# An attention layer with a mixture of experts on one core: new orders at four places, and a front with the keys' bias as a column of the weights' product, the high parts of u first, the output bias added by VectorE, and statistics moved

## The chip, the core and the metric

The kernel runs on one core of a Trainium2 chip. Five engines work from queues of their own and meet at semaphores: TensorE (PE, matmuls and transposes into PSUM), VectorE (DVE), ScalarE (ACT, activations and scaled copies), GpSimd (POOL), and SyncE (SP, which here only issues transfers). The metric is the device time of one execution in microseconds (us), lower is better. A median over several executions is given beside one profiled execution.

## What is computed

```python
x = L0_attn_x                                   # (4, 1024, 256), float32
xn = _layernorm(x, axis=-1)
q, k, v = xn @ Wq.T + bq, xn @ Wk.T + bk, xn @ Wv.T + bv
qk = q @ k.T                                    # no scaling
theta = 0.5 + 0.2 * sigmoid(qk) + 0.15 * tanh(qk) + 0.1 * relu(qk)
s = softmax(theta) @ v @ Wo.T + bo
expert = argmax(xn @ Wr + br)                   # one of 8 per token
y = gelu(xn @ W1[expert] + b1[expert]) @ W2[expert] + b2[expert]   # hidden width 1024
out = x + s * silu(y)
```

## The kernel before

**Arithmetic.** Every large product is made from two-part numbers: a high part in TensorE's reduced fp32 (`_hi`, `_h`) and the remainder (`_lo`, `_l`), and three matmuls (`product`, lines 855, 856, 857) give high·high, high·low and low·high. High parts are copies, most of them by ScalarE; low parts are subtractions by VectorE. Scores are not made from q and k: the kernel forms `M = Wq.T Wk` once, `u = M.T xn` for a batch, and a tile of scores is u times xn. What the biases add to a score is a term per query that softmax can't see except through sigmoid, tanh and relu: `r_col` (from bq and Wk, added to u), a column of offsets `c_all` per token (from bk and Wq, which stands as an extra column `E` of the router's weights `small_w`), and the scalar `kappa` (bq times bk). `G = (Wo Wv).T` stands for value and output projection together, `attn_const` for their biases.

**Stages.** 32 tiles of 128 tokens, 8 to a batch. Batch 0 comes first, while the front still makes its constants and the layer norm of the other batches: statistics by VectorE (`row_statistics`, `variances`, `scales`), the scaling by ScalarE, VectorE and, for the batches 1 to 3, GpSimd (`normalize`). While batch 0's tiles 1 to 3 are scored, the normalised rows of the batches 3, 2 and 1 are transposed in between (`turn`, line 1011; copied out of PSUM by ScalarE's `keep_turned`) and routed (`route`; VectorE's `take_turned` reads the logits and gives `c_ready`). Tokens are then sorted by expert. The expert phase works through units of 256 sorted tokens (`hidden`, `expert_out`); the last unit of an expert with at most 128 tokens is a **half unit** (`half_rows`, `half_turned`, `half_out`, with ScalarE's `gelus_half` and VectorE's `parts_half`), whose hidden values come out by token and are transposed before the Gelu. After the experts come the batches 1 to 3 (tiles 8 to 31): `scores(n + 1)`, `transposes(n)` of the exponentials, a job for the next batch, `weighted(n - 1)` (line 855 `v_hi,pT_hi`), with ScalarE's `acts` (two tanh and a relu on each half of a tile of scores) and `exps`, and VectorE's `thetas`, `transposed_parts` and `finish`.

**Order.** Everything is written by hand: each engine has one program (`@block.tensor` and so on), and the order of the statements is the order of the engine's queue; an engine that waits for a semaphore holds up all that stands behind it. The tiles in `ROUTING` let ScalarE make the first half of `pT_hi` too, which otherwise VectorE makes. ScalarE holds one set of function tables at a time; a dummy activation on `warm` brings in the next set (Sqrt, Exp with Tanh, Gelu). Tile 8's scores are made before the expert phase, and its `acts` and `thetas` run inside the last expert (`tile_8`).

## Time and profile before

| | us |
|---|---|
| median of 3 runs (lowest, highest) | 537.14 (536.58, 537.76) |
| the profiled execution, its own time | 537.1 |
| its span from first to last instruction | 535.4 |
| TensorE busy in the span | 517.5 (97%) |
| VectorE busy | 408.2 (76%) |
| ScalarE busy | 335.2 (63%) |
| GpSimd busy | 195.4 (36%) |

The profiled execution's time is 1.7 us more than its span and equals the median within 0.1 us. Busy time of TensorE counts the overlapping ends of pipelined matmuls, so 97% busy does not exclude small gaps. In the rows below, a duration in brackets is how long the engine had been idle before the row, with what ended the wait.

### The profile page before, as it was taken

The page shows a single profiled execution, that of the slowest core. Times are in us where ns is not written, and L with a number is a line of the kernel's source. Part 1 is how long each engine was busy: PE and PEld are TensorE (multiplying, and loading weights), DVE is VectorE, ACT ScalarE, POOL GpSimd, SP SyncE. Part 2 cuts the span into 40 slices and gives each one's busy share as a digit, 9 for nine tenths or more (in the row PEclk, how much of TensorE's full clock was granted, in tenths as well). Part 3 has the DMA queues.
Part 4 walks back from the last instruction along what each step waited for, and adds up shares of the span by engine and source line. Part 5 has one row for each costly group of instructions (what it writes and reads, how often), then busy time and mean ns, then how long its engine had stood idle before and what let it go on. Part 6 is the DMA issues. An engine that isn't in the chain of part 4 may idle for free.

```text
span 535.4 us, 10760 instructions
## 1 busy us (share of the span) xinstructions
PE 517.5 (97%) x3779; PEld 484.8 (91%) x3779; DVE 408.2 (76%) x810; ACT 335.2 (63%) x611; POOL 195.4 (36%) x230
## 2 busy tenths in 40 slices
PE   7998999999999999999999979999999999999996
PEld 6888899899989999899999969988899988999996
DVE  6897688955758855498555688758999999777896
ACT  3488778535536634266334464678777887877882
POOL 2226337931222212322112222004577685343443
PEclk9999999999999999999999999999999999999999
DMA  8942920027314731145311421005123232211121
GB/s 279 352 160 99 353 81 1 1 51 245 118 60 131 233 111 39 60 131 206 138 39 39 130 72 40 22 21 184 56 97 106 73 118 90 61 48 41 60 61 59
DMA packets 40323, 57.09 MB, mean 107 GB/s; under 512 B 3607, under 2 KB 35358, under 8 KB 39726
## 3 DMA queue, kind: packets, MB, share of 16 engines
q1 hardware_dynamic: 35020, 45.62, 25.5%
q0 software_dynamic: 3488, 9.47, 6.1%
q10 hardware_dynamic: 1762, 1.32, 0.8%
q8 instruction: 29, 0.48, 0.4%
q14 instruction: 24, 0.20, 0.1%
HBM read 40.68 MB, written 17.56 MB: 109 GB/s over the span
## 4 chain that ended last, share of the span: by engine, by line
PE 83%; DVE 8%; ACT 5%; issue 2%; DMA 2%; ACTq 0%; POOL 0%; POOLq 0%; DVEq 0%
PE ps L855 25%; PE ps L857 24%; PE ps L856 24%; PE ps L954 5%; DVE stats L1316 1%; PE ps L1137 1%; PE ps L1021 1%; DMA row<-xn_rows,unit_token 1%; ACT hid L731 1%; PE ps L1011 1%; DVE theta L1374 1%; DVE theta L1370 1%; DMA xn_all<-in_L_attn_x_dram 1%; ACT theta L618 1%; ACT theta L608 1%
## 5 line engine op out<-in xcount | busy, mean ns | idle before, releaser
L855 PE MATMUL ps<-v_hi,pT_hi 128*128 128x258 f32 x256 | 76.4, 298 | 2.2 <-issue 0.8
L856 PE MATMUL ps<-v_lo,pT_hi 128*128 128x258 f32 x256 | 72.4, 283 | 0.0
L717 ACT ACTIVATE hid<-ps,b_now 128x256 f32<-128x256 f32 x128 | 53.6, 471 | 30.0 <-PE ps L857 29.1
L857 PE MATMUL ps<-v_hi,pT_lo 128*128 128x258 f32 x256 | 72.2, 282 | 0.0
L1370 DVE SCALAR_TENSOR_TENSOR theta<-tanh_s,theta 128x512 f32<-128x512 f32 x64 | 48.8, 763 | 20.7 <-ACT tanh_s L609 20.0
L618 ACT ACTIVATE theta<-theta,neg_max 128x512 f32<-128x512 f32 x64 | 42.9, 721 | 29.9 <-DVE neg_max L1374 29.8
L855 PE MATMUL ps<-w_hi_even,hidT_h 128*128 128x256 f32 x200 | 58.1, 290 | 3.2 <-DVE hidT_l L1658 3.2
L739 ACT ACTIVATE g_sb<-y_sb 128x512 f32<-128x512 f32 x20 | 12.6, 632 | 71.7 <-DVE y_sb L1663 71.7
L499 POOL COPY unit_token<-sorted_token 128x2 int32 x19 | 3.7, 195 | 147.1 <-PE ps L1137 147.1
L857 PE MATMUL ps<-w_hi_even,hidT_l 128*128 128x256 f32 x200 | 56.6, 283 | 0.0
L856 PE MATMUL ps<-w_lo_even,hidT_h 128*128 128x256 f32 x200 | 56.6, 283 | 0.0
L608 ACT ACTIVATE theta<-ps,c_half 128x512 f32<-128x512 f32 x64 | 44.2, 691 | 15.9 <-PE ps L857 15.9
L855 PEld LDWEIGHTS ps<-v_hi,pT_hi 128*128 128x128 f32 x256 | 48.3, 189 | 4.7 <-issue 3.3
L506 POOL DMA_INDIRECT g_tile<-sorted_g,slot_g x32 | 37.7, 1177 | 38.8 <-DMA sorted_g<-g_sb 33.6
L855 PE MATMUL ps<-xnT_hi,u_hi 128*128 128x512 f32 x128 | 51.8, 404 | 0.0
L490 POOL DMA_INDIRECT row<-xn_rows,unit_token x38 | 43.4, 1141 | 20.7 <-POOL unit_token L499 14.9
L857 PE MATMUL ps<-xnT_hi,u_lo 128*128 128x512 f32 x128 | 50.2, 392 | 0.0
L856 PE MATMUL ps<-xnT_lo,u_hi 128*128 128x512 f32 x128 | 49.9, 390 | 0.0
L856 PE MATMUL ps<-rowT_l,w_hi_even 128*128 128x256 f32 x176 | 49.8, 283 | 0.0
L855 PE MATMUL ps<-rowT_h,w_hi_even 128*128 128x256 f32 x176 | 49.8, 283 | 0.0
L857 PE MATMUL ps<-rowT_h,w_lo_even 128*128 128x256 f32 x176 | 49.8, 283 | 0.0
L856 PEld LDWEIGHTS ps<-v_lo,pT_hi 128*128 128x128 f32 x256 | 48.5, 190 | 0.3
(248 smaller groups left out, 1648.6 us busy)
## 6 DMA issues: line engine op xcount, KB each, us to landing
w_raw_odd<-in_L_ffn_W_dram SPq DMA_DIRECT2D x10, 1024.0 KB, 5.7
w_raw_even<-in_L_ffn_W_dram SPq DMA_DIRECT2D x6, 1024.0 KB, 6.5
sorted_g<-g_sb SPq DMA_DIRECT2D x20, 256.0 KB, 2.2
xn_rows<-xn_all SPq DMA_DIRECT2D x4, 1024.0 KB, 6.1
x_tile<-in_L_attn_x_dram SPq DMA_DIRECT2D x32, 128.0 KB, 2.2
out_dram<-g_tile SPq DMA_DIRECT2D x32, 128.0 KB, 1.7
xn_all<-in_L_attn_x_dram SPq DMA_DIRECT2D x3, 1024.0 KB, 12.4
kept_xT<-passing_xT SPq DMA_DIRECT2D x2, 1024.0 KB, 4.1
```

What stands on the lines that cost most here:

```text
L490: pool.indirect_dma_start(row[:, a, :], None, xn_rows, bass.IndirectOffsetOnAxis(ap=tokens[:, a:a + 1], axis=0)).then_inc(row_in, 16)
L506: pool.indirect_dma_start(g_tile[:, p % RING, :], None, sorted_g, bass.IndirectOffsetOnAxis(ap=slot_g[:, n:n + 1], axis=0)).then_inc(g_in[ ...
L608: nc.scalar.activation(theta[:, j % 2, cols], bank, ACT.Tanh, bias=c_half[:, n:n + 1], scale=0.5)
L618: nc.scalar.activation(part, part, ACT.Exp, bias=neg_max[:, j % 2, 1:2], scale=-1.0).then_inc(exp_done, 1)
L717: last = nc.scalar.activation(hid[:, j % 2, c * UNIT:(c + 1) * UNIT], ps[:, HID_BANK + j, c * UNIT:(c + 1) * UNIT], ACT.Gelu, bias=b1_now[ ...
L731: last = nc.scalar.activation(half_gelus(s)[:, c - first, :], ps[:, HID_BANK + 2 + c // 4, c % 4 * P:(c % 4 + 1) * P], ACT.Gelu, bias=b1_n ...
L739: nc.scalar.activation(g_sb[:, :, :], y_sb[:, :, :], ACT.Tanh, scale=0.5).then_inc(y_tanh, 1)
L855: mm(dst, a_hi, b_hi, start=first, stop=False)
L856: mm(dst, a_hi, b_lo, start=False, stop=False)
L857: return mm(dst, a_lo, b_hi, start=False, stop=last)
L954: last = nc.tensor.transpose(ps[:, PT_BANK + h, i * P:(i + 1) * P], theta[:, n % 2, h * HALF + i * P:h * HALF + (i + 1) * P], ident[:, :])
L1370: v.scalar_tensor_tensor(part, tanh_s[:, cols], KT, part, ALU.mult, ALU.add).then_inc(mixed, 1)
```

## The change

The changed kernel does the following; it computes the same outputs.

- **Front.** The rows of the three biases are loaded first on ScalarE's queue, and their transposition stands ahead of TensorE's eight warm-up matmuls. VectorE writes bk as column `D` of `wk_raw`, so the product M has 257 columns and its last one is what `offset_products` made before; `kappa` is a VectorE reduction over two broadcast rows (`bq_all`, `bk_all`, two new transfers of 128 KB on SP's queue). `first_u` issues high·high, then low M, then the transpositions of batch 0's second half, then low xn. ScalarE takes over the normalisation of tiles 4 and 5, `bv_wide` and the copy `woT`. The output bias is a broadcast tile halved by GpSimd and added by VectorE instead of a matmul, and the product for `attn_const` stands behind G. Batch 2's eight row statistics, which stood ahead of `thetas(0, [0])`, move: two go behind it, six behind `attn_const`.
- **Turned batches.** VectorE's `take_turned(0)` stands behind two `low_v` instead of three. ScalarE copies bank 6 before bank 7 (`KEPT_ORDER`), and TensorE waits for three copies, not four, before `values`.
- **Half units.** Gelu and splitting go in four steps of two chunks. ScalarE makes `hidT_h` of the steps 2 and 3 (copies); VectorE makes only `hidT_l` there. The wait for the first half of W1's low part moves from ahead of the branch on the kind of unit to inside it.
- **Last expert.** `tile_8` has the Exp table and `exps(8)`; a load of Gelu follows, and Exp again behind `acts(9)`.
- **End.** The tiles 30 and 31 are in `ROUTING`; `thetas(31)` is not split; tile 31 is transposed, into score banks, between the halves of `values(30)`; GpSimd waits for `theta_done` of tile 31 before it works on tile 28.

The diff, cut to its core:

```diff
-    ROUTING = (3, 4, 5, TPB)
+    ROUTING = (3, 4, 5, TPB, NT - 2, NT - 1)
+        def pT_bank(n, h):
+            return ps[:, (S_BANK if n == NT - 1 else PT_BANK) + h, :]
+        KEPT_ORDER = [(0, 1), (3, 2)]
@@ sync
-            for first, src in ((BQ, bq), (BK, bk), (BV, bv)):
-                sp.dma_start(bias_rows[first:first + DC, :], src.rearrange("(c p) -> c p", p=P)).then_inc(small_in, 16)
+            for kept, src in ((bq_all, bq), (bk_all, bk)):
+                sp.dma_start(kept[:, :], src.rearrange("(a d) -> a d", a=1).to_broadcast([P, D])).then_inc(pairs_in, 16)
@@ gpsimd
             normalize(range(3 * TPB, 4 * TPB))
+            pool.wait_ge(bo_in, 16)
+            nc.gpsimd.tensor_scalar(bo_all[:, :], bo_all[:, :], 0.5, 0.0, ALU.mult, ALU.add).then_inc(bo_halved, 1)
...
+                if n == NT - 4:
+                    pool.wait_ge(theta_done, NT)
                 pool.wait_ge(half_s_ready, n + 1)
@@ scalar
+            for first, src in ((BQ, bq), (BK, bk), (BV, bv)):
+                act.dma_start(bias_rows[first:first + DC, :], src.rearrange("(c p) -> c p", p=P)).then_inc(small_in, 16)
             act.dma_start(wq_raw[:, :, :], chunked(Wq)).then_inc(wqk_in, 16)
...
                     for h in range(2):
                         if n < 3:
-                            for q in range(2 * h, 2 * h + 2):
+                            for q in KEPT_ORDER[h]:
                                 keep_turned(n, q)
...
             def gelus_half(u, par):
-                nc.scalar.activation(hid[:, 0, :], ps[:, HID_BANK, :], ACT.Copy).then_inc(gelu_done, 1)
-                for s in range(1, 4):
+                nc.scalar.activation(hid[:, 0, :], ps[:, HID_BANK, :], ACT.Copy).then_inc(act_kept, 1)
+                for s in range(4):
...
+                last.then_inc(act_kept, 1)
+                wait_apart(act, act_kept, u * 2 + 2)
+                for s in range(2, 4):
+                    nc.scalar.activation(hidT_h[:, 2 * s:2 * s + 2, 0:P], half_gelus(s), ACT.Copy).then_inc(gelu_done, 1)
...
                 for h in range(2):
                     acts(TPB, h)
+                nc.scalar.activation(warm[:, 2:3], zeros[:, 0:1], ACT.Exp)
+                exps(TPB)
...
+            nc.scalar.activation(warm[:, 3:4], zeros[:, 0:1], ACT.Gelu)
             with act.If(last_u < full_7):
                 gelus(last_u, 1)
             with act.If(full_7 < last_u + 1):
                 gelus_half(last_u, 1)
-            nc.scalar.activation(warm[:, 3:4], zeros[:, 0:1], ACT.Exp)
-            exps(TPB)
             for h in range(2):
                 acts(TPB + 1, h)
+            nc.scalar.activation(warm[:, 3:4], zeros[:, 0:1], ACT.Exp)
@@ tensor
+            def first_u():
...
+                pe.wait_ge(M_high, DC)
+                for k in range(DC):
+                    pe.wait_ge(lnT_hi, k + 1)
+                    for q in range(2):
+                        one(q, k, M_hi, xnT_hi[0], start=k == 0, stop=False)
+                pe.wait_ge(M_ready, DC)
+                for k in range(DC):
+                    for q in range(2):
+                        one(q, k, M_lo, xnT_hi[0], start=False, stop=False)
+                turn_0(2)
+                turn_0(3)
+                for q in range(2):
+                    for k in range(DC):
+                        pe.wait_ge(lnT_lo, k + 1)
+                        last = one(q, k, M_hi, xnT_lo[0], start=False, stop=k == DC - 1)
...
                 if n < 3:
-                    pe.wait_ge(turned_kept, 4 * n + 4)
+                    pe.wait_ge(turned_kept, 4 * n + 3)
...
             def units(e):
-                pe.wait_ge(w1_split, split - 1)
...
-            weighted(NT - 2)
+            pe.wait_ge(half_s_ready, NT - 3)
+            values(NT - 2, blocks=range(0, TPB // 2))
+            pe.wait_ge(acts_done, (NT - 1) * 2)
             transposes(NT - 1)
+            values(NT - 2, blocks=range(TPB // 2, TPB))
             weighted(NT - 1)
@@ vector
+            dve.wait_ge(biasT_done, 1)
+            v.tensor_copy(wk_raw[:, :, D], ps[:, 6, BIAS_COL + BK:BIAS_COL + BK + DC]).then_inc(bias_kept, 1)
+            v.tensor_copy(bias_cols[:, :], ps[:, 6, BIAS_COL:BIAS_COL + 3 * DC]).then_inc(bias_kept, 1)
             dve.wait_ge(x0_in[0], 16)
...
             transposed_parts(0)
-            for q in range(3):
+            for q in range(2):
                 low_v(0, q)
             take_turned(0)
-            low_v(0, 3)
+            for q in range(2, 4):
+                low_v(0, q)
...
+            thetas(TPB + 1)
             biased(last_u, 1)
-            thetas(TPB + 1)
             transposed_parts(TPB)
```

**Where instructions stand, first place.** TensorE's queue at the start of the program, before: the warm-ups (`ident` times `ident`), M (`wk_raw,wq_raw`), the transposed bias rows, batch 0's first rows, `r_col`'s product, and then u with the offsets' products in it.

```order
L862 MATMUL ps<-ident 128x128 [waits masks_ready]
L866 MATMUL ps<-wk_raw,wq_raw 128x256 [waits wqk_in]
L871 MATMUL ps<-ident,bias_rows 128x6 [waits small_in]
L882 MATMUL ps<-ident,xn_all 128x128 [waits xn_pool,xn_dve,xn_act]
L893 MATMUL ps<-bias_cols,wk_raw 128x48 [waits bias_kept]
L855 MATMUL ps<-xnT_hi,M_hi 128x512 [waits lnT_lo,M_ready]
L856 MATMUL ps<-xnT_lo,M_hi 128x512
L857 MATMUL ps<-xnT_hi,M_lo 128x512
L901 MATMUL ps<-bias_cols,bq_wide 128x48 [waits wide_ready]
L901 MATMUL ps<-bias_cols,bq_wide 128x48
L893 MATMUL ps<-bias_cols,wq_raw 128x48 x4
L855 MATMUL ps<-xnT_hi,M_hi 128x512 [waits lnT_lo]
```

The same queue in the changed kernel:

```order
L892 MATMUL ps<-ident,bias_rows 128x6 [waits small_in,masks_ready]
L895 MATMUL ps<-ident 128x128 x8
L900 MATMUL ps<-wk_raw,wq_raw 128x257 [waits wqk_in,bias_kept]
L923 MATMUL ps<-bias_cols,wk_raw 128x48 x4
L912 MATMUL ps<-ident,xn_all 128x128 [waits xn_pool,xn_dve,xn_act]
L933 MATMUL ps<-xnT_hi,M_hi 128x512 [waits lnT_hi,M_high]
L933 MATMUL ps<-xnT_hi,M_hi 128x512 [waits lnT_hi]
L933 MATMUL ps<-xnT_hi,M_lo 128x512 [waits M_ready]
L912 MATMUL ps<-ident,xn_all 128x128 [waits xn_pool,xn_dve,xn_act]
L933 MATMUL ps<-xnT_lo,M_hi 128x512 [waits lnT_lo] x4
L1091 MATMUL ps<-ident,wo_raw 128x128 [waits wo_in]
```

The bias rows now stand ahead of everything, the offsets' products (lines 901 and 893 with `wq_raw`) are gone, and the first u waits for high parts alone.

**Second place.** VectorE's queue from tile 0's last maximum to batch 3's offsets, before (`stats` are row statistics, `logits`, `c_all` and `c_half` are `take_turned`):

```order
L1533 TENSOR_SCALAR attn_const<-ps 128x256 [waits const_done]
L1316 BN_STATS stats<-xn_all 128x6 [waits x_in1]
L1316 BN_STATS stats<-xn_all 128x6 x7
L1323 BN_AGGR mean_var<-stats 128x2 x15
...
L1356 TENSOR_TENSOR v_lo<-ps,v_hi 128x2x256 [waits v_high] x3
L1500 TENSOR_TENSOR logits<-ps,br_all 128x8x8 [waits logits_done]
L1361 TENSOR_SCALAR c_all<-ps,kappa 128x8 [waits dve_step]
L1362 TENSOR_SCALAR c_half<-c_all 128x8 [waits dve_step]
L1356 TENSOR_TENSOR v_lo<-ps,v_hi 128x2x256 [waits v_high]
```

And in the changed kernel:

```order
L1560 SCALAR_TENSOR_TENSOR attn_const<-ps,bo_all 128x256 [waits bo_halved,const_done]
L1353 BN_STATS stats<-xn_all 128x6 x6
L1353 BN_STATS stats<-xn_all 128x6 [waits x_in1]
L1353 BN_STATS stats<-xn_all 128x6 x7
L1360 BN_AGGR mean_var<-stats 128x2 x15
...
L1393 TENSOR_TENSOR v_lo<-ps,v_hi 128x2x256 [waits v_high] x2
L1524 TENSOR_TENSOR logits<-ps,br_all 128x8x8 [waits logits_done]
L1398 TENSOR_SCALAR c_all<-ps,kappa 128x8 [waits dve_step]
L1399 TENSOR_SCALAR c_half<-c_all 128x8 [waits dve_step]
L1393 TENSOR_TENSOR v_lo<-ps,v_hi 128x2x256 [waits v_high] x2
```

Six statistics came in ahead of the variances, and the offsets moved ahead of one subtraction of v.

**Third place.** TensorE's queue at the end of the program, before (tile 30's products, tile 31's transpositions, tile 31's products):

```order
L857 MATMUL ps<-v_hi,pT_lo 128x258
L954 MATMUL ps<-ident,theta 128x128 [waits exp_done]
L954 MATMUL ps<-ident,theta 128x128 x3
L954 MATMUL ps<-ident,theta 128x128 [waits exp_done]
L954 MATMUL ps<-ident,theta 128x128 x3
L855 MATMUL ps<-v_hi,pT_hi 128x258 [waits pT_ready,half_s_ready]
```

And in the changed kernel, where twelve more products of tile 30 follow the last row:

```order
L886 MATMUL ps<-v_hi,pT_lo 128x258
L997 MATMUL ps<-ident,theta 128x128 [waits exp_done,acts_done]
L997 MATMUL ps<-ident,theta 128x128 x3
L997 MATMUL ps<-ident,theta 128x128 [waits exp_done]
L997 MATMUL ps<-ident,theta 128x128 x3
L884 MATMUL ps<-v_hi,pT_hi 128x258 [waits pT_ready]
```

The transpositions moved up by half of tile 30's products.

## Rows read from the trace of the kernel before

**Rows 1.** The page: the span, and TensorE's busy time.

```profile
span 535.4 us, 10760 instructions
...
PE 517.5 (97%) x3779; PEld 484.8 (91%) x3779; DVE 408.2 (76%) x810; ACT 335.2 (63%) x611; POOL 195.4 (36%) x230
```

**Rows 2.** Waits of TensorE: us in total, times, longest.

```profile
PE ps L855 <- DVE hidT_l L1658: 3.2, 6, 0.7
```

**Rows 3.** Transfers, their size and us from issue to landing.

```profile
wq_raw<-in_L_attn_Wq_dram ACTq DMA_DIRECT2D x1, 256.0 KB, 4.0
...
wv_raw<-in_L_attn_Wv_dram ACTq DMA_DIRECT2D x1, 256.0 KB, 8.4
```

**Rows 4.** Timeline, 0 to 30 us: start, duration, engine, line, tiles.

```profile
2.92 3.79 PE L862 MATMUL ps<-ident 128*128 128x128 f32 x16 [2.92 <-POOL ident L429]
...
12.24 0.54 PE L901 MATMUL ps<-bias_cols,bq_wide 128*128 128x48 f32 x4
...
24.43 1.03 PE L1065 MATMUL ps<-woT,bv_wide 128*128 128x256 f32 x4
...
25.39 0.69 PE L1066 MATMUL ps<-bo_row,ones 1*128 1x256 f32 x2
```

**Rows 5.** Timeline, 33 to 53 us, VectorE, GpSimd, TensorE, ScalarE.

```profile
33.60 2.71 DVE L1316 BATCH_NORM_STATS2 stats<-xn_all 128x6 f32<-128x256 f32 x8
...
41.37 8.65 POOL L446 TENSOR_SCALAR xn_all<-xn_all,rstd,shift 128x256 f32<-128x256 f32 x16 [11.70 <-DVE shift L1331]
...
43.30 1.29 DVE L1356 TENSOR_TENSOR v_lo<-ps,v_hi 128x512 fp32r<-128x512 f32 x2
...
44.89 0.47 PE L855 MATMUL ps<-xnT_hi,u_hi 128*128 128x512 f32 x1
...
46.97 0.63 PE L1011 MATMUL ps<-ident,xn_all 128*128 128x128 f32 x4 [1.14 <-DVE c_half L1362]
...
50.97 1.10 ACT L563 ACTIVATE passing_xT<-ps 128x512 f32<-128x512 f32 x2
...
52.17 0.36 PE L855 MATMUL ps<-v_hi,pT_hi 128*128 128x258 f32 x1 [0.30 <-issue]
```

**Rows 6.** Timeline, 153 to 157 us: the first half unit.

```profile
153.30 2.17 ACT L731 ACTIVATE hid<-ps,b_now 128x128 f32<-128x128 f32 x8 [1.21 <-PE ps L1193]
...
155.51 0.61 DVE L1656 CAST hidT_h<-hid 128x512 fp32r<-128x512 f32 x1
...
156.16 0.77 DVE L1658 TENSOR_TENSOR hidT_l<-hid,hidT_h 128x512 fp32r<-128x512 f32 x1
...
156.98 0.39 PE L855 MATMUL ps<-w_hi_even,hidT_h 128*128 128x256 f32 x1 [0.49 <-DVE hidT_l L1658]
```

**Rows 7.** Timeline, 319 to 322 us: the last expert's weights.

```profile
319.32 2.34 DVE L1686 TENSOR_TENSOR w_lo_odd<-w_raw_odd,w_hi_odd 128x1024 fp32r<-128x1024 f32 x2
...
321.62 0.38 PE L855 MATMUL ps<-rowT_h,w_hi_odd 128*128 128x256 f32 x1 [1.08 <-issue]
```

**Rows 8.** Timeline, 352 to 369 us: from the experts to batch 1.

```profile
352.59 1.28 ACT L829 ACT_TABLE_LOAD   x1
...
353.99 1.32 ACT L618 ACTIVATE theta<-theta,neg_max 128x512 f32<-128x512 f32 x2
...
360.78 0.36 PE L855 MATMUL ps<-v_hi,pT_hi 128*128 128x258 f32 x1 [0.72 <-DVE pT_lo L1388]
...
368.37 1.09 PE L954 MATMUL ps<-ident,theta 128*128 128x128 f32 x8 [0.82 <-DVE pT_lo L1390]
```

**Rows 9.** Timeline, 525 to 529 us: the last tile.

```profile
525.21 1.11 DVE L1374 CUSTOM_DVE_ANT_0 theta<-theta,relu_s,neg_max 128x512 f32<-128x512 f32 x1
...
526.36 1.34 ACT L618 ACTIVATE theta<-theta,neg_max 128x512 f32<-128x512 f32 x2 [3.63 <-DVE neg_max L1374]
...
527.14 1.27 PE L954 MATMUL ps<-ident,theta 128*128 128x128 f32 x8 [0.49 <-ACT theta L618]
...
528.86 0.36 PE L855 MATMUL ps<-v_hi,pT_hi 128*128 128x258 f32 x1 [0.46 <-DVE pT_lo L1801]
```

243 lines of the change are left out of this document (109 added, 134 removed).

## The prediction

> **What bounds the kernel now.** I read the page first: TensorE is busy 97% of a span of 535.4 us [rows 1]. Busy time there counts overlapping ends, so I then went through the starts of its instructions in the timeline and compared each distance with the usual one for that pair of shapes. That leaves some 25 us in which TensorE could have gone on and did not, spread over the whole program, in pieces of at most 1.3 us. The kernel is bound by what TensorE has to issue; only these pieces and TensorE's own instructions can be won, and the waits view names their ends: VectorE's low parts of hidden values in half units (3.2 us idle in 6 waits, [rows 2]), the offsets of batch 3 at 46.97 [rows 5], ScalarE's copies at 52.17 [rows 5], the last expert's W1 at 321.62 [rows 7], the passage to batch 1 at 360.78 and 368.37 [rows 8], and the end [rows 9]. From 60 to 150 and from 370 to 520 us there is hardly a gap, so a lead of TensorE won early is kept: ScalarE and VectorE are driven by its scores there.
>
> **Front, to 33 us.** The offsets' products go: 0.54 us for `bq_wide` [rows 4] and twice as many records with wq, about 1.1 us. The row product of bo (25.39 to 26.01, 0.62 us) goes too, and the product before it (24.43, [rows 4]) moves behind G, so G begins 1.58 us earlier relative to its surroundings. Against that: the warm-ups last 3.79 us and start at 2.92 [rows 4]; now they wait for the bias rows. The first transfer on ScalarE's queue lands 4.0 us after issue for 256 KB [rows 3]; three transfers of 1 KB should take some 1.8 us after the third's issue at about 1.4, my estimate from the 4.0 less its data time (256 KB at the 150 to 180 GB/s of one of two queues). So the warm-ups start at about 3.5 and M 0.6 us later than before. The second half of batch 0 is requested 0.9 us later too, which holds statistics, normalisation and `turn_0(2)` until about 13.6. By adding up the new queue in the same durations I get tile 0's u done and the second u jobs begun about 0.95 us earlier than before. Column 257 costs one column in 257, nothing I can see. The moved halves (tiles 4 and 5, woT, bv_wide) go from a VectorE that is full between 20 and 40 us to a ScalarE with room: hidden. Scores of tile 1 then start about 1.6 us earlier.
>
> **What decides is VectorE behind that.** The last maximum of tile 0 follows G by a fixed chain (high G, low G, offsets, theta), so it ends about 0.95 + 1.58 = 2.5 us earlier than 33.3. But six statistics come in there: the row at 33.60 has 8 in 2.71 us, 0.34 each [rows 5], 2.0 us; adding bo costs nothing beside a multiplication (both read PSUM once). So thetas(1), the scales of batches 2 and 1 and low v begin only 0.4 us earlier. TensorE has run ahead and waits for two low v, before tile 2's scores: 44.25 instead of 44.89 [rows 5]. The order is worth more: the offsets come after two of the four `low_v` (0.65 us each, from 1.29 for two, [rows 5]), and are done at about 45.0, before TensorE reaches the transposition. What is late next is GpSimd: its 16 rows take 8.65 us from 41.37, so the eighth ends at 45.7 [rows 5], with the start 0.4 earlier at 45.3. The transposition of 46.97 [rows 5] thus moves to 45.3: **1.7 us** for the whole front. From below: if the early part gains nothing, the order alone gives 46.97 − 45.7 = 1.3; if the second half of x lands late enough to push the variances by 1 us, 0.3. From above: 2.2.
>
> **Kept order.** At 52.17 `values` waits for both copies of 50.97, 1.10 us together [rows 5]. The copy of bank 6, which `values` writes, ends first now, 0.55 earlier; the router's product needs the other only after the first three matmuls. TensorE's idle there is 0.30 in the row and 0.45 by the starts. It comes twice (tiles 1 and 2): **0.8 us**, bounds 0.4 and 1.0.
>
> **Half units.** In the first one ScalarE ends its eight Gelus at 155.47 (153.30 + 2.17), VectorE then casts 512 columns (0.61) and subtracts (0.77), and TensorE, out of work at 156.33, goes on at 156.98 [rows 6]. Now ScalarE copies 256 columns (0.35 to 0.4, from the 0.6 of its 512-column copies) and VectorE subtracts 256 (half of 0.77, 0.42): 155.47 + 0.1 + 0.4 + 0.42 + 0.1 = 156.5. That is **0.5 us** in each of two such units; the Gelu's first step and its 0.7 us wait stay. What ScalarE does more (0.7 us) delays the next row's high part, which still has 1 us of cover. The third stands at 316 and is followed by 321.62: VectorE's first half of W1 is ready at 320.5 (319.32 + half of 2.34), and TensorE starts 1.08 us after the last thing that it waited for [rows 7], because it takes the branch and its loads behind that wait. With the wait inside the branch this goes. But the two copies of ScalarE push the high part of W1 and so the low part by 0.45, to 320.95; TensorE starts at 321.0: **0.6 us** for this unit and its successor together. Bounds of the three: 0.6 and 2.1.
>
> **Passage to batch 1.** Today ScalarE loads the Exp table at 352.59, behind the last Gelus, and exps(8) start 353.99, 1.4 us later [rows 8]. Now exps(8) stand in `tile_8`, where ScalarE idles for 2 us, but a load of Gelu comes behind them and one of Exp behind acts(9): two more loads, 2 × 1.28 and a dummy of 0.2 each. The first two loads lie in front of the last half unit: its first copy moves from 347.3 to about 349.3 and ends at 349.9, when TensorE reaches its transposition at 349.76, so 0.15 us is lost. Behind it acts(9) begin at 353.6 instead of 355.2, the high parts of tile 8 at 358.5 (before 358.6, since the third load is ahead of them), low parts at once, as `thetas(9)` are done: the wait at 360.78 (0.72, [rows 8]) goes. The next wait, at 368.37 (0.82, [rows 8]), hangs on acts(10), which follow exps(9) and the gate and come 0.45 us earlier: so of all this only about **0.3 us** reaches the tiles behind. Bounds: a loss of 1, and 1.2.
> On a switch of tables the trace shows 1.28 us for the load and 1.4 from the last Gelu to the first exponential [rows 8]. The Trainium skill (ScalarE: Activation LUTs, What ACT_TABLE_LOAD costs) puts a switch at about 2.66 us, with some 1.38 of drain beside a load of 1.28. By the rows the two added switches are covered; by that rule both early ones take 2.5 us more together, and the half unit's copy comes that much after TensorE. The row speaks against the rule.
>
> **End.** Tile 31's second maximum takes 1.11 us at 525.21 [rows 9] against 0.69 elsewhere, beside GpSimd's tile 28, which now waits; and VectorE no longer splits `thetas(31)` around tile 30's parts. By the same durations theta is done at about 523.2, not 526.3, the exponentials at 524.6 (1.34, [rows 9]), and the transpositions stand in the middle of values(30), at 525.4 to 526.3, with the parts of tile 31 made beside its second half. The waits for 527.14 and 528.86 [rows 9] go, 1.5 us with the second transposing chain. New is that values(30) waits for its own low parts, behind thetas(31), some 0.45. Tile 31's products start at about 527.8 instead of 528.86: **1.05 us**. Bounds: 0.3 and 1.5. GpSimd then does tile 28, the last gather and tile 29 from 523.2; that gather must land by 529.6, and should at 528.
>
> **Sum.** 1.7 + 0.8 + 1.0 + 0.6 + 0.3 + 1.05 = 5.45 us off the profiled execution's 537.1, which equals the median: **531.6 us**. Nothing else on TensorE changes.
>
> **The rivals.**
> *The front passes nothing on.* The added 0.9 us on the second half of x, and 256 KB of broadcast rows ahead of the other batches, hold VectorE, whose chain to 41.37 then starts no earlier or later. For it: TensorE's gain there is already spent on six statistics but for 0.4 us. The front gives 0.2, the sum 3.95: 533.1 us.
> *The switches cost what the rule says.* The last half unit waits 1.9 us more: 533.5 us, nearer 534 with the 0.3 gone.
> *ScalarE is the worse splitter, or GpSimd is late at the end.* ScalarE waits for its own Gelus before the copies, and if that costs 0.5 us, half units give 0.2; or tile 31's g is gathered only after tile 28 and lands past 529.6, which takes the end's 1.05. Each leaves 532.7 to 533.
> *Slower: the bias rows land late.* VectorE now holds its whole queue, statistics of x included, and TensorE warm-ups and M, for one small transfer. Were it as late as `wv_raw`, 8.4 us after issue [rows 3], it would land at 9.8, M would start 3.6 us of warm-ups later, at 13.4, instead of the 7.1 that I reckon (3.5 + 3.6), and the front would be 6.3 us later: 531.6 + 6.3 = 537.9 us. It decides from about 9 us of landing. Against it: that row had three large transfers ahead in its queue, and the new ones have none.
> *No change,* with these gains turned into waits of TensorE elsewhere: the stretches 60 to 150 and 370 to 520 speak against it: 536.5.
>
> **Chances.** Forecast (531 to 532.5) 0.55; front passes nothing on 0.14; table rule 0.06; splitter or GpSimd 0.10; more than reckoned, all upper bounds together 529 to 530.5, 0.07; slower 0.04; no change 0.04. A change of 0.2% (1.1 us) is about what can be told from none here. Faster 0.92, same 0.04, slower 0.04. The range leaves out the last two and the far part of the better case: 529.8 to 534.4 us.
>
> **What would show it.** M starting about 7.1 against 6.5 before (right) or past 8 (bias rows late); the transposition of 46.97 at 45 to 45.6, ended by GpSimd or nothing; no wait at 52.17's successor; half units' second wait at 0.1 to 0.2 instead of 0.65; first products of the last expert within 0.2 us of W1's low part; table loads of 1.28 with no idle around them; tile 31's transpositions ahead of half of tile 30's products, and less than 0.6 us of waits after 520. I would be wrong if ScalarE between 344 and 361 us falls behind TensorE, or if VectorE's idle before 40 us shows that x came later than it could work.

## The result

The changed kernel takes **540.76 us** (median of 4 runs, 540.06 to 540.84) against 537.10 us (536.58 to 537.76) for the kernel before on the same chip: ratio 1.0068, 95% interval 1.0057 to 1.0080. It is 3.7 us slower. I had forecast 531.6 us in a range of 529.8 to 534.4, and gave "slower" a chance of 0.04. The profiled execution took 540.8 us with a span of 539.1 us.

The page of the changed kernel, its span and its engines (compare [rows 1]):

```profile
span 539.1 us, 10813 instructions
...
PE 516.4 (96%) x3765; PEld 485.0 (90%) x3765; DVE 402.6 (75%) x801; ACT 343.8 (64%) x629; POOL 195.3 (36%) x231
```

PE issues 14 products fewer and is busy 1.1 us less, as the change promises, and the span is 3.7 us longer. So the time went into waits or behind PE's end. I compared the starts of the same PE instructions in the two traces. The changed kernel's lateness, in us by which the same instruction starts later than before, reads at successive places: +1.18 at the first turn of expert rows (122.55 before, 123.73 after); +1.44 at the second, a gather that came late; +0.98 and +0.52 behind the first two half units; +0.23 at the third one's first products and -0.22 at its last ones; **+3.15 behind the last expert's first unit**; +2.26 in the steady part of the later batches; +1.17 at PE's last product (which ends at 532.0 before, 533.1 after); **+3.73 at the end of the span**. Half units, passage and PE's end gained; the front, one place at 320 us, and what stands behind PE's end lost. Each of the three has its rows. A single trace stands for its kernel only to some 0.5 us: the profiled run of the kernel before, 537.1, lies 0.45 above the median of the 27 runs of it beside the last experiments.

**The front.** Transfers of the changed kernel, first 9 us, with KB and us from issue to landing (compare [rows 3]):

```profile
xn_all<-in_L_attn_x_dram ACTq DMA_DIRECT2D x1, 512.0 KB, 10.7
...
wq_raw<-in_L_attn_Wq_dram ACTq DMA_DIRECT2D x1, 256.0 KB, 8.2
bq_all<-in_L_attn_bq_dram SPq DMA_DIRECT2D x1, 128.0 KB, 6.0
```

Timeline of the changed kernel, PE, 0 to 17 us (compare [rows 4]; M stood at 6.50 before):

```profile
5.33 0.24 PE L892 MATMUL ps<-ident,bias_rows 6*128 6x6 f32 x1 [5.33 <-DMA bias_rows<-in_L_attn_bv_dram]
5.50 3.78 PE L895 MATMUL ps<-ident 128*128 128x128 f32 x16
10.35 1.98 PE L900 MATMUL ps<-wk_raw,wq_raw 128*128 128x257 f32 x8 [1.06 <-DMA wq_raw<-in_L_attn_Wq_dram]
```

Wq lands 8.2 us after its issue instead of 4.0, the bias rows land at about 5.3, and M starts at 10.35, 3.85 us later than before and 3.25 later than the 7.1 that I reckoned. The lateness is 2.83 at 18 us and 1.25 at G's first product: 1.58 of it goes with the two products that stood ahead of G, as forecast. For the 1.0 before that the rows don't separate the offsets' products that are gone from the new order of u.

Batch 0's rows came late as well, and would have been next in line. ScalarE now issues ten transfers before it computes, until 8.1 us instead of 4.9, and VectorE waits for its first square root. ScalarE's first row in the kernel before, then the changed kernel:

```profile
4.95 1.28 ACT L541 ACT_TABLE_LOAD   x1 [4.95 <-issue]
```

```profile
8.13 1.28 ACT L557 ACT_TABLE_LOAD   x1 [8.13 <-issue]
...
9.76 0.18 DVE L1367 RECIPROCAL rstd<-std 128x4 f32<-128x4 f32 x1 [1.91 <-ACT std L561]
```

The first half of batch 0 is normalised from 10.17 instead of 7.87. Then VectorE is late. Timeline of the changed kernel, 34 to 54 us (compare [rows 5]):

```profile
34.66 4.66 DVE L1353 BATCH_NORM_STATS2 stats<-xn_all 128x6 f32<-128x256 f32 x14
...
44.06 9.09 POOL L456 TENSOR_SCALAR xn_all<-xn_all,rstd,shift 128x256 f32<-128x256 f32 x16 [12.17 <-DVE shift L1368]
...
45.80 1.28 DVE L1393 TENSOR_TENSOR v_lo<-ps,v_hi 128x512 fp32r<-128x512 f32 x2
...
47.13 0.50 PE L884 MATMUL ps<-xnT_hi,u_hi 128*128 128x512 f32 x1 [0.73 <-DVE v_lo L1393]
```

Fourteen statistics stand there instead of eight, GpSimd starts its rows 2.7 us later than before, and PE waits for two `v_lo`.

**The last expert.** Timeline of the changed kernel at 320 us (compare [rows 7]), then the branch of line 1283, the jump into the last expert's loop (shortest, median and longest in ns, first and last start):

```profile
319.88 2.36 DVE L1718 TENSOR_TENSOR w_lo_odd<-w_raw_odd,w_hi_odd 128x1024 fp32r<-128x1024 f32 x2 [0.26 <-ACT w_hi_odd L607]
...
323.30 0.36 PE L884 MATMUL ps<-rowT_h,w_hi_odd 128*128 128x256 f32 x1 [2.98 <-issue]
```

```profile
L1283 PEldq COMPARE_BRANCH  x3: 67/234/3826, 319.2 to 346.7; - x3
```

In the kernel before, the same branch (line 1250 there):

```profile
L1250 PEldq COMPARE_BRANCH  x3: 67/219/664, 320.8 to 343.6; - x3
```

W1's first low half is there at 321.1; nothing else is awaited; the jump alone takes 3.83 us instead of 0.66, from 319.20 to 323.03. "Issue" in the wait is this. And it costs twice. Windows of the changed kernel (busy time and number of instructions for PE, PEld, DVE, ACT, POOL; then granted clock, DMA share, GB/s):

```profile
321.00:323.00 2.00, 0.00 (x0) 0.00 (x0) 2.00 (x3) 1.78 (x3) 0.00 (x0) 1.00 0.03 4
323.00:327.50 4.50, 4.21 (x23) 4.24 (x23) 3.37 (x6) 1.47 (x3) 0.00 (x0) 0.62 0.17 58
327.50:331.00 3.50, 3.50 (x33) 3.50 (x31) 2.30 (x5) 1.86 (x5) 0.00 (x0) 1.00 0.02 8
```

TensorE had been idle for 2.98 us. It is granted 1.2 GHz instead of 2.4 from 323.6 to 327.0: its products start 0.214 us apart, not 0.12, 1.5 us lost over 16 of them. The page gives a mean clock of 0.993 against 0.999 or 1.0 in runs of the kernel before.

**The close.** The sequencer rows of the program's last line, changed kernel, then before:

```profile
L53 POOLq DRAIN  x1: 6887/6887/6887, 532.0 to 532.0; - x1
```

```profile
L52 POOLq DRAIN  x1: 6819/6819/6819, 528.2 to 528.2; - x1
```

Now GpSimd's last addition starts at 532.0, since tile 30 is divided behind tile 31's transpositions. Its close ends at 538.9, while the last output has landed at 536.1. From PE's end to the span's end it is 5.9 us now and was 3.4: 2.6 us lost.

### The profile page after: what moved, and what is told of

It is laid out like the page before. It is cut to its first block, busy times and chain, and to the rows that moved or that the text cites. A ratio compares the mean times of both kernels' runs of the same rounds, so it can differ in the third digit from the quotient of the medians.

```text
span 539.1 us, 10813 instructions
## 1 busy us (share of the span) xinstructions
PE 516.4 (96%) x3765; PEld 485.0 (90%) x3765; DVE 402.6 (75%) x801; ACT 343.8 (64%) x629; POOL 195.3 (36%) x231
## 4 chain that ended last, share of the span: by engine, by line
PE 82%; DVE 6%; ACT 5%; DMA 3%; issue 2%; POOL 1%; ACTq 1%; POOLq 0%; DVEq 0%
PE ps L884 25%; PE ps L886 24%; PE ps L885 24%; PE ps L997 5%; DMA xn_all<-in_L_attn_x_dram 2%; DVE stats L1353 2%; PE ps L1173 1%; PE ps L1062 1%; DMA row<-xn_rows,unit_token 1%; ACT theta L621 1%; ACT tanh_s L622 1%; ACT hid L753 1%; POOL xn_all L456 1%; PE ps L1052 1%; DVE theta L1407 1%
## 5 line engine op out<-in xcount | busy, mean ns | idle before, releaser
L1407 DVE SCALAR_TENSOR_TENSOR theta<-tanh_s,theta 128x512 f32<-128x512 f32 x64 | 47.5, 742 | 23.5 <-ACT tanh_s L622 22.8
```

Source lines behind the costliest of these rows:

```text
L1407: v.scalar_tensor_tensor(part, tanh_s[:, cols], KT, part, ALU.mult, ALU.add).then_inc(mixed, 1)
```

## The experiments

All ratios are to the kernel before on the same chip; expectations were written ahead. "Jump" is the branch into the last expert's loop.

### The end

**e1**: tile 30's last two operations on VectorE.

```diff
-                if p + 1 == NT:
-                    break
+                if p + 2 >= NT:
+                    continue
...
+            v.tensor_tensor(near, half_s[:, (n - 1) % 2, :], near, ALU.mult).then_inc(near_scaled, 1)
...
+            v.tensor_tensor(near, near, x_near, ALU.add).then_inc(near_ready, 1)
```

> The changed kernel, with tile 30's last multiplication and addition done by VectorE instead of GpSimd, so that GpSimd's last work is tile 29's addition. Theory (GpSimd's close): in the changed kernel GpSimd's last addition starts at 532.0, the drain that closes its program takes 6.89 us from there, and the span ends at 539.1 behind it, though the last output landed at 536.07. Here GpSimd's close begins near 529.2 and ends near 536.0, and the span ends by the last output, 536.1 to 536.5: time 537.9 to 538.3 (2.6 below the changed kernel's 540.8). Rival: the span's last 3 us are something else at the program's end (an output that is recorded late, the closing of another engine), and the time stays at 540.6 to 541. Second rival: VectorE's two more operations push its last three, and 0.5 to 1 of the gain is lost.

Measured 537.59 us (535.84 to 538.94, 10 runs), ratio 1.0016 (1.0004 to 1.0028). GpSimd's close begins at 528.3:

```profile
L53 POOLq DRAIN  x1: 6837/6837/6837, 528.3 to 528.3; - x1
```

It ends at 535.2, the span at 535.8, behind PE's end (532.4) by the kernel before's 3.4 us. The first theory holds: 2.5 us of the close are gone. The time is 3.2 us less than the changed kernel's, 0.3 below the range, and the rest of it comes from PE's end, 0.8 earlier with a jump of 3.27 instead of 3.83. Its single runs spread by 3.1 us: the one at 535.84 had a granted clock of 1.000, the others 0.995 to 0.997.

**g4**: the new end alone, on the kernel before.

```diff
-            weighted(NT - 2)
+            pe.wait_ge(half_s_ready, NT - 3)
+            values(NT - 2, blocks=range(0, TPB // 2))
+            pe.wait_ge(acts_done, (NT - 1) * 2)
             transposes(NT - 1)
+            values(NT - 2, blocks=range(TPB // 2, TPB))
...
-            thetas(NT - 1, [0])
...
+            thetas(n)
+            transposed_parts(n - 1)
```

> The kernel before, with only the new end (tile 30's values split around tile 31's transpositions, VectorE's thetas(31) in one, GpSimd's wait at tile 28). Theory (GpSimd's close): PE ends 1.1 earlier (530.9 instead of 532.0), the last output lands 1.1 earlier, but tile 30 is divided only now at about 528.8, GpSimd's last addition starts at 529.8 instead of 528.25, and its close takes 6.9 from there: span 536.7, time 538.4, 1.3 slower than before though PE ends earlier. Rival (PE's end decides): 535.9.

Measured 538.25 us, ratio 1.0024 (1.0014 to 1.0033); profiled: PE's end 531.1, 0.9 earlier than before, and the close from 529.9 for 6.9 us, span 537.0. It came as expected. An end that is 1.1 us quicker on PE (lateness +0.15 at 520 us, -0.92 at PE's end) makes the kernel 1.3 us slower.

**i2**: the best kernel below (f3) without GpSimd's wait at tile 28.

```diff
-                if n == NT - 4:
-                    pool.wait_ge(theta_done, NT)
```

> The kernel with the front of before, slot 128 and tile 30's last operations on VectorE (533.11), without GpSimd's new wait at tile 28. Theory (the prediction's reason for the wait): GpSimd's multiplication beside VectorE's last maximum lengthens it from 0.69 to 1.11, tile 31's theta comes 0.4 later, but its transpositions now have half of tile 30's products as cover: PE's end moves by 0 to 0.4, time 533.1 to 533.5. Rival (the wait protects nothing and only delays GpSimd's gathers): 532.7 to 533.1.

Measured 533.63 us (533.13 to 534.11), f3 533.11 (532.87 to 533.58). In the trace the first half of tile 31's maximum takes 1.12 us instead of 0.69, and tile 30's first products wait 0.59 instead of 0.27. The wait is worth some 0.3 to 0.5 us, about what the theory said (its range ended at 533.5), and the loss of the changed kernel is not its doing.

### The jump

**e2**: the wait for W1 back ahead of PE's branches.

```diff
+                pe.wait_ge(w1_split, split - 1)
                 with pe.If(u0 < full):
```

> The changed kernel, with the wait for the first half of W1 back ahead of the branch on PE (as in the kernel before), for all experts. Theory (the jump): in the changed kernel PE's branch into the last expert's loop stands in the trace with 3.83 us (before: 0.66), and nothing else was awaited; it began at 319.2, before the wait, right behind the products before it, so the loop's code had not been brought in. With the wait ahead PE comes to the branch at about 321.1, it takes 0.7, first product at 322.1, PE is idle 2 us instead of 3.2 and TensorE's clock stays at 2.4 GHz: 1.15 + 1.4 = 2.5 less, time 538.2. Rival (the place of the code): the jump costs 3.8 us because the changed program's code lies elsewhere, whatever waits ahead: first product near 324.9, time 541 to 543. Rival (no part in the end): the 2.5 us at 330 are taken up later, time 540.8.

Measured 543.38 us, ratio 1.0121 (1.0104 to 1.0138): 2.6 us *slower* than the changed kernel. The jump starts at 321.1 and takes 3.69 all the same. My theory, that PE only came too early, is refuted; the first product starts at 324.91, as the rival had it.

**g1**: the new half units alone, on the kernel before.

```diff
-                for s in range(1, 4):
+                for s in range(4):
...
+                for s in range(2, 4):
+                    nc.scalar.activation(hidT_h[:, 2 * s:2 * s + 2, 0:P], half_gelus(s), ACT.Copy).then_inc(gelu_done, 1)
```

> The kernel before, with only the new half units (ScalarE splits one half, four steps of two columns of blocks; the wait for W1 stays ahead of the branch). Theory (each half unit gives 0.45, and the shifted code of the third one makes the jump long): 0.45 less at each of the first two half units, 0.3 at the third, then the jump into the last expert's loop takes 3.3 to 3.9 us in the trace instead of 0.66 and its 16 KB are fetched only behind it: 537.0 - 1.2 + 2.6 to 4.2 = 538.4 to 540. Rival (the jump's length comes from another part of the change: the wait moved inside, the passage, the end): jump 0.66, time 535.8 to 536.2.

Measured 541.54 us, ratio 1.0081 (1.0064 to 1.0098). PE gains 0.46 and 0.45 at the first two half units, 0.29 ahead of the third one's transpositions and 0.45 more within it, then jumps for 3.71 us:

```profile
L1254 PEldq COMPARE_BRANCH  x3: 67/234/3706, 320.1 to 347.8; - x3
```

Windows of this kernel, same columns as above:

```profile
320.00:323.00 3.00, 0.00 (x0) 0.00 (x0) 3.00 (x4) 1.69 (x4) 0.00 (x0) 0.75 0.02 5
323.00:328.00 5.00, 4.07 (x19) 4.08 (x20) 1.63 (x3) 1.25 (x3) 0.00 (x0) 0.50 0.17 57
```

PE is idle for nearly 5 us, with 1.2 GHz granted from 321.5, while it is still idle, to 328.3: this one part costs 4.6 us by itself. That is 1.5 above my range: I had the jump right, but not the length of the slow clock, nor 0.6 us lost at 361 (see i4).

**g2**: only the wait moved inside the branch, on the kernel before.

```diff
-                    if c == HC // 2:
-                        pe.wait_ge(w1_split, split)
+                    if c % (HC // 2) == 0:
+                        pe.wait_ge(w1_split, split - 1 + c // (HC // 2))
...
-            pe.wait_ge(w1_split, split - 1)
             with pe.If(u7 < last_u):
```

> The kernel before, with only the wait for the first half of W1 moved from ahead of PE's branch to the expert's first product. What I had predicted for it: first product of the last expert within 0.2 of W1's first low half (320.5), so 0.9 earlier than 321.62: time 536.1 to 536.4. Rival (arriving early at the branch, PE's jump now waits for the fetch of its code itself): the jump takes 2 to 3.8, first product at 321.5 to 323.3, time 537 to 540.

Measured 536.73 us, ratio 0.9997 (0.9987 to 1.0007): no difference. The first product gains 0.6 against its surroundings, and the jump is half long:

```profile
L1247 PEldq COMPARE_BRANCH  x3: 67/219/1662, 319.6 to 343.4; - x3
```

Neither expectation fits, and what is won is within the measurement. The transfers of instructions, below, explain the 1.66.

**i1**: one more wait in the old half unit.

```diff
                     for c in range(*HALF_STEPS[s]):
+                        if c == 6:
+                            pe.wait_ge(hidT_ready, u * 4 + s + 3)
```

> The kernel before, with one more wait on PE in the half units: the two last blocks of the second product wait again for the value for which the two before them have waited, so that nothing is awaited that is not there. The half units' new code has as many instructions on PE as the old (51 rows in each), so the jump into the last expert's loop is not long because code has moved; what differs is where PE's sequencer is held. Theory (held sequencer): in the kernel before the sequencer runs ahead through the last four blocks and asks for the next 16 KB at 318.40, before the jump at 320.80; with a wait in the middle of them it is held, asks only at the jump, and the jump takes 3.3 to 3.9: time 539.5 to 541.5, as with the new half units alone. Rival (it is the later splitting of the data that holds it, not the wait's place): jump 0.66, time 536.9 to 537.1.

Measured 536.82 us, ratio 1.0005 (0.9996 to 1.0014), jump under 0.4. A wait in that place does not make the jump long. But the trace shows as many PE instructions as that of the kernel before, where g1's shows one more; so this run does not exclude that g1's code has moved across the border of a block.

**f1**: the changed kernel, loop head moved.

```diff
-                             head_slot={mybir.EngineType.PE: 0}) as u:
+                             head_slot={mybir.EngineType.PE: 128}) as u:
```

> The changed kernel with one number changed: the last expert's loop on PE begins at slot 128 of a block of instructions instead of slot 0, so that the jump into it stays in the block in which the sixth expert's code ends. Theory (place of the code): the trace shows PE's 16 KB of instructions fetched at 320.29, 1.1 us after the jump at 319.20 began, in the changed kernel, and at 318.40, before the jump, in the kernel before; with the target in a block that is there the jump takes 0.2 to 0.4, the first product starts by W1's first low half at 321.2 instead of 323.30, PE is idle about 1.2 instead of 3.2 and the clock stays at 2.4 GHz: 2.1 + 1.4 = 3.5 less, time 537.3. Rival (the jump is long whatever its target): 540.6 to 541. Rival (the loop, now across a block's border, pays a fetch on its second turn): gain under 1.5, time above 539.

Measured 538.22 us (537.38 to 540.29), ratio 1.0031 (1.0021 to 1.0041): 2.5 us less for one number, 0.9 short of the 537.3 expected. PE's end lies 2.9 us ahead of the changed kernel's. No jump of this loop is longer than 0.29 us now, and PE waits for data:

```profile
L1283 PEldq COMPARE_BRANCH  x3: 67/233/286, 319.3 to 343.9; - x3
```

```profile
321.32 0.35 PE L884 MATMUL ps<-rowT_h,w_hi_odd 128*128 128x256 f32 x1 [0.93 <-DVE w_lo_odd L1718]
```

0.6 us of it are lost again by the loop's second turn. My rival laid that to a fetch, but no branch there is long: PE waits 0.24 and 0.30 us for hidden values, at 329.2 and 330.3. It looks as if ScalarE and VectorE do not follow what PE wins at the head of the unit; no run tests that.

**i3** and **i4**: the same edit on the kernel before, and on g1.

```diff
-                             head_slot={mybir.EngineType.PE: 0}) as u:
+                             head_slot={mybir.EngineType.PE: 128}) as u:
```

> The kernel before, with the last expert's loop at slot 128 alone. Theory (the block is there, but here it was nearly in time anyway): jump 0.2 to 0.4 instead of 0.66, 0.3 to 0.4 gained at the first product, 0.6 lost on the loop's second turn (327.5 to 339.4 in the two kernels with this slot): time 536.9 to 537.3, no gain. Rival (the slot is a gain of its own, and the 533.11 owes part to it): under 536.4.

> The new half units alone on the kernel before (541.54), with the last expert's loop at slot 128. Theory (all of that loss is the jump): first product of the last expert at about 321.2 to 321.6, the half units' 0.45 + 0.45 + 0.3 stay, less 0.6 on the loop's second turn: time 536.0 to 536.5. Rival (ScalarE's two more copies push W1's high and low parts, and with them the last expert): 536.8 to 538.

i3: 536.67 us, ratio 0.9999 (0.9990 to 1.0008), so the slot is no gain of its own in the time; in the one trace PE wins 0.5 at the last expert and, against my theory, keeps it through the loop's second turn. i4: 536.89 us, ratio 0.9999 (0.9990 to 1.0009), against g1's 1.0081: all of g1's loss goes with the jump. But the three half units' gain does not arrive either, as the rival had it. The trace shows it won by 320 us, then no gain at the last expert (ScalarE's copies push W1: PE waits 1.52 for it before 321.17, in i3 0.59 before 321.14), and 0.6 lost at 361, where PE waits 1.32 instead of 0.72 [rows 8] because the last half unit has kept ScalarE from tile 9.

The transfers of instructions (16 KB each, queue q8) settle the kind of cause. Kernel before, 316.5 to 320.7 us, ahead of the jump:

```profile
q8 instruction: 1, 0.02, 2.3%
```

The changed kernel has none between 316.5 and 319.2, and its next one begins at 320.29, 1.1 us after the jump has begun. From the traces, in us:

| | transfer | jump | jump's end behind the transfer's |
|---|---|---|---|
| kernel before | 318.40 to 319.94 | 320.80 to 321.46 | 1.52 |
| g2 | 318.87 to 319.91 | 319.56 to 321.22 | 1.31 |
| changed kernel | 320.29 to 321.56 | 319.20 to 323.03 | 1.48 |
| g1 | 321.14 to 322.30 | 320.07 to 323.77 | 1.48 |
| e2 | 322.40 to 323.28 | 321.07 to 324.76 | 1.48 |

In the other four kernels with a long jump (e1, e3, e4, f2) the last column is 1.32 to 1.48 too. So the jump's length follows from when its block has come: long, half long and 0.66 are one thing. The Trainium skill (Runtime: NRT & Kernel Launch, Instruction fetch mechanics) says that prefetch is sequential in blocks of 256 instructions, and that a taken branch to a block that isn't there waits for a transfer; these rows and f1 agree. Why the old half unit has the block asked for 2.4 us ahead, and the new one, with one more PE instruction in the whole trace, only at the jump, none of the runs shows.

### The front

**e3**: the broadcasts of bq and bk behind the loads of x.

```diff
-            for kept, src in ((bq_all, bq), (bk_all, bk)):
-                sp.dma_start(kept[:, :], ...).then_inc(pairs_in, 16)
             for b in TURNED:
                 load_x(b * TPB, TPB, x_in[b])
+            for kept, src in ((bq_all, bq), (bk_all, bk)):
+                sp.dma_start(kept[:, :], ...).then_inc(pairs_in, 16)
```

> The changed kernel, with the two transfers that repeat bq and bk over 128 partitions issued behind the loads of x of batches 3 to 1 instead of ahead of them. Theory (broadcasts): these 256 KB in 1 KB pieces, issued at the same time as Wq and the second half of x, hold them: Wq landed at 10.21 in the changed kernel (4.79 before), x's second half at 13.14 (7.94 before). Moved, Wq lands at 6 to 8 and x's second half at 9 to 10; M then starts behind the warm-ups at 9.3 instead of 10.35, and batch 0's products, 1.2 to 1.5 later than before throughout, gain 1.0 to 1.5: time 539.3 to 539.8. Rival (the bias rows): the three small transfers ahead of Wq on ScalarE's queue hold it; Wq still lands near 10.2, time 540.6 to 541.

Measured 540.34 us, ratio 1.0056 (1.0040 to 1.0073), within the spread of the changed kernel. Wq still lands at 10.5, x's second half at 13.4. The theory that the broadcasts as such hold Wq is refuted. That the 1 MB of x, now next on SyncE's queue, takes their place is possible and was not tested.

**f2**: Wq ahead of the bias rows, warm-ups ahead of their wait.

```diff
+            act.dma_start(wq_raw[:, :, :], chunked(Wq)).then_inc(wqk_in, 16)
             for first, src in ((BQ, bq), (BK, bk), (BV, bv)):
                 act.dma_start(bias_rows[...], ...).then_inc(small_in, 16)
-            act.dma_start(wq_raw[:, :, :], chunked(Wq)).then_inc(wqk_in, 16)
```

> The changed kernel with Wq's transfer issued ahead of the three bias rows on ScalarE's queue (behind them in the changed kernel), and PE's eight warm-up products ahead of the wait for the bias rows. Theory (order of the queue): Wq lands near 4.8 as before instead of 10.21, the bias rows near 6, M starts at 7 to 7.5 instead of 10.35, x's second half lands at 8.5 to 9.5 instead of 13.14; then the front comes out as I had reckoned it, 1.2 to 1.7 ahead of the kernel before instead of 1.2 to 1.5 behind: time 537.6 to 538.4. Rival (the transposed bias and the two broadcasts hold M anyway): M at 9 to 10, time 539.5 to 540.5. Rival (the front passes nothing on, G and the third batch's statistics set batch 0): 539.3 to 539.6, no better than the front of before.

Measured 539.12 us, ratio 1.0052 (1.0033 to 1.0072). A transfer of f2, and PE's start of M in its timeline:

```profile
wq_raw<-in_L_attn_Wq_dram ACTq DMA_DIRECT2D x1, 256.0 KB, 4.2
```

```profile
7.44 0.22 PE L894 MATMUL ps<-ident,bias_rows 6*128 6x6 f32 x1 [0.73 <-DMA bias_rows<-in_L_attn_bv_dram]
8.06 2.00 PE L900 MATMUL ps<-wk_raw,wq_raw 128*128 128x257 f32 x8 [0.40 <-DVE bias_cols L1471]
```

The order of the queue is the cause of the late Wq; by what mechanism three transfers of 1 KB cost it 5.4 us stays open. But the bias rows then land at 7.4, five us after issue with nothing large ahead but Wq, and M waits for them. So does VectorE, whose queue has the bias columns ahead of the statistics of x: these start at 7.92 instead of 5.17, and PE waits for batch 0's rows, which it transposed at 9.02 before. Timeline of f2, 0 to 17 us:

```profile
7.92 1.40 DVE L1353 BATCH_NORM_STATS2 stats<-xn_all 128x6 f32<-128x256 f32 x4
...
11.76 1.09 PE L912 MATMUL ps<-ident,xn_all 128*128 128x128 f32 x8 [0.87 <-ACT xn_all L565]
```

Batch 0 comes out 0.3 us ahead of the kernel before, not 1.2 to 1.7. The time, with a jump of 3.99 in it, lies between the first theory and the last rival.

**e4**: the changed kernel with the whole front of the kernel before; of the diff against that one, for instance,

```diff
-            for first, src in ((BQ, bq), (BK, bk), (BV, bv)):
-                act.dma_start(bias_rows[...], ...).then_inc(small_in, 16)
...
-            r_product()
             turn_0(0)
             turn_0(1)
-            first_u()
...
+            u_product(0, 0)
+            u_product(0, 1)
```

> The changed kernel with the whole front of the kernel before (its transfers, constants, M, u, statistics up to batch 1); kept are the order of the kept quarters, the half units, the wait inside the branch, the passage to batch 1 and the end. Theory (a front that costs): batch 0's products stand 1.2 to 1.5 earlier, all else as in the changed kernel: time 539.3 to 539.6. Rival (the front costs nothing in the end, the rest does): 540.6 to 540.9. If the jump into the last expert's loop depends on where the code lies, it may come out short here, and 2.5 more are gained: 536.9 to 537.1; the trace tells it by PE's branch near 318.

Measured 538.50 us (536.95 to 540.36, 10 runs), ratio 1.0033 (1.0021 to 1.0046): 2.3 us less than the changed kernel, and 0.8 below what I expected. The jump is long here too (3.51). Single runs spread by 3.4 us: the three with a granted clock of 0.999 took 536.95 to 537.56, the seven at 0.991 to 0.994 took 538.4 to 540.4. The wait of 2.7 us before the last expert sometimes costs the clock and sometimes not.

**h1**: f4 (below) with batch 2's eight statistics back in their old place.

```diff
             for q in range(2, 4):
                 low_u(0, q)
+            dve.wait_ge(x_in[2], 16)
+            row_statistics(range(2 * TPB, 3 * TPB))
...
-            row_statistics(range(2 * TPB, 2 * TPB + 2))
...
-            row_statistics(range(2 * TPB + 2, 3 * TPB))
```

> The changed kernel with all three cures, and the eight statistics of batch 2 back ahead of tile 0's theta (where the kernel before has them; the changed kernel has two behind the first half of thetas(0) and six behind the constants). Theory (six statistics hold VectorE): in the kernel with the three cures G stands 0.07 later than before, yet tile 2's scores wait 0.91 at 45.95 for VectorE's v_lo and the first transposition behind them 0.49, while the front of before with the new kept order stands 0.84 earlier there. With the statistics back the 0.91 goes and tile 1's theta starts 1.5 to 2 earlier: time 533.4 to 533.8. Rival (the statistics only change place on VectorE's one queue): tile 0's last maximum comes 2 later, the wait at tile 2's scores stays, time 534.2 to 534.8. Rival (they now stand in the chain of G's low part): slower, above 535.

Measured 534.04 us (533.56 to 534.29), f4 534.42 (533.70 to 535.12): no more than 0.4 us. The wait for `v_lo` at 45.95 is gone, but the first transposition stands at 46.85 and waits for the offsets:

```profile
46.85 0.63 PE L1055 MATMUL ps<-ident,xn_all 128*128 128x128 f32 x4 [0.55 <-DVE c_half L1402]
```

Neither the theory (533.4 to 533.8) nor the rival (534.2 to 534.8) is excluded.

### All three cures

**f3**: front of before, slot 128, tile 30 on VectorE. **f4**: the changed front with Wq first, and the same two. Their edits are those of e1 and f1 on e4 and on f2.

> The changed kernel with the front of before, the last loop at slot 128 and tile 30's last two operations on VectorE. PE ended at 529.3 with the front of before (532.0 in the kernel before) with a jump of 3.51 in it. If the three causes add up: 2.1 less for the jump, the end 3.4 behind PE's as in the kernel before: span 530.4 to 530.8, time 532.1 to 532.5, 0.991 of before, and runs within 0.5 of one another instead of 3.4 (with the front of before they spread from 536.95 to 540.36, those above 538 at a granted clock of 0.991 to 0.994). Rival (each cure uncovers another wait): 533.5 to 535.

> The changed kernel with all three cures: Wq first, the last loop at slot 128, tile 30's last two operations on VectorE. If the causes are separate and add up: 540.8 - 3.5 (jump and clock) - 2.6 (GpSimd's close) - 2.4 to 2.9 (Wq) = 531.8 to 532.3, what I had predicted for the change itself. If the changed front is no better than that of before: as the kernel with the front of before, 532.1 to 532.5. Rival: the sum falls short by over 1, which leaves a cause that is not among the three.

f3: **533.11 us** (532.87 to 533.58), ratio **0.9931** (0.9918 to 0.9945). f4: 534.42 us, ratio 0.9950 (0.9936 to 0.9964). Both are faster than either kernel, f3 by 3.7 us than the kernel before on the same chip. Page and first turn of f3:

```profile
span 531.2 us, 10837 instructions
...
PE 518.0 (98%) x3779; PEld 485.5 (91%) x3779; DVE 404.8 (76%) x808; ACT 342.4 (64%) x625; POOL 193.4 (36%) x228
```

```profile
46.13 0.63 PE L1028 MATMUL ps<-ident,xn_all 128*128 128x128 f32 x4 [0.17 <-DVE c_half L1380]
```

f3 falls short of its expected 532.1 to 532.5 by at least 0.6 us, f4 of its 531.8 to 532.3 by at least 2.1: by the difference of the two, the changed front is 1.3 us slower than the old one even with Wq first. At G's first product the two traces are level (+0.13 in f3, +0.07 in f4); at the first turned rows they lie 1.1 us apart (-0.84, +0.27). The difference arises behind G, on VectorE.

One thing stands beside this in the profiled run of f4, PE, 2 to 14 us:

```profile
8.95 3.47 PE L903 MATMUL ps<-wk_raw,wq_raw 128*128 128x257 f32 x8 [0.40 <-DVE bias_cols L1474]
```

M takes 3.47 us where f2 takes 2.00, its products 0.43 us apart instead of 0.22: TensorE runs at half the pace there, after a wait of 1.58 for the bias rows. The profile's clock column has 1.00 for this stretch, so that it is the clock is argued from the pace alone. It is so in h1 (3.80) and e3 (3.77) too, and in part even with the old front (2.86 in f3, 3.05 in e4). At G it is worth little: in h1, where M starts 0.1 after f2's and takes 1.8 more, G is 0.13 later; in e3 it is at most 0.6 against the changed kernel.

## Why the prediction was wrong, point by point

Forecast and measurement lie 9.2 us apart: front and kept order together 3.7 (2.5 gained against 1.2 lost), a late gather 0.3, the first two half units 0.1, the third and the last expert 3.2, the end 2.5, less 0.6 that the passage gave more. Three steps carry it: the landing of bias rows and Wq in the front, the 1.08 "issue" taken for a fixed price of PE's branch, and GpSimd's last work, whose close I didn't look at.

**Front, predicted 1.7 us gained; measured 1.2 us lost by 122 us, 0.3 of kept order taken in.** Two steps failed. I took the bias rows to land at 3.2, 1.8 after their last issue, from "the 4.0 less its data time"; they landed at 5.3, and at 7.4 behind Wq (f2). And I had only counted the bias rows' issues as 0.9 us of delay for what stands behind them in the queue, when Wq landed 5.4 us later than before and x's second half 5.2. I priced "the bias rows land late" as a rival and gave it 0.04, but tied it to the rows alone; what came late in the changed kernel was Wq behind them. f2 takes that away, and then the rival's own mechanism shows, M and VectorE's whole queue held by the bias rows. f3 against f4 shows that the new front still has no gain to give. Of the 2.5 us by which G was to come earlier, the 1.58 of the two products held (1.68 in f2, 1.58 in f4), and the 0.95 of the early part failed: at 18 us u is 1.28 late in f2 and 1.65 in f4. So G is not early at all (-0.30 and +0.07), and the six statistics, which left "only 0.4 us" of it in my sum, stand on VectorE with nothing won ahead of them. The one thing at 46.97 that came as forecast was the order of `low_v` and offsets: with the old front the wait of 1.14 there is 0.17, and the transposition stands at 46.13, 0.84 earlier.

**Kept order, predicted 0.8; measured 0.3.** The waits at 52.17 and 64.95 are gone in f3 and in the changed kernel, but the wait for the offsets ahead of tile 2's transposition grows from 0.17 at 59.75 to 0.55 (at 58.94 in f3, 61.25 in the changed kernel), and the next one takes the rest.

**Half units, predicted 0.5 + 0.5, and 0.6 for the third with the last expert; measured 0.46 + 0.46, then 0.3 and 0.45 at the third and 3.4 lost at the last expert, 2.6 lost for the two together.** Timeline of the changed kernel's first one (compare [rows 6]):

```profile
157.03 0.72 ACT L761 ACTIVATE hidT_h<-hid 128x256 fp32r<-128x256 f32 x2
...
157.95 0.19 PEld L884 LDWEIGHTS ps<-w_hi_even,hidT_h 128*128 128x128 f32 x1 [0.23 <-DVE hidT_l L1689]
```

ScalarE copies right behind its last Gelu, and PE's wait of 0.49 [rows 6] is gone but for 0.23 at its weight load: the mechanism and size of the first two were right, and the third gives the same 0.45. For the third and the last expert together I had 0.6, with the wait inside the branch. g2 shows the gain at the first product, and that it is no gain in the time: in f1 and f3 too PE wins that 0.6 at the last expert's head and loses it again by its second unit, behind hidden values. The failed step is the reading of 1.08 "issue" [rows 7] as what PE's branch and loads cost behind that wait, so that it would go with the wait; 0.66 of it was a jump that was still waiting for its block (the block had come at 319.94, the jump ended at 321.46). That the jump could get longer was in no rival.

**Passage, predicted 0.3; measured 0.9.** Timeline of the changed kernel, ScalarE at 348 us (compare [rows 8]):

```profile
346.82 0.74 ACT L623 ACTIVATE relu_s<-ps,c_all 128x512 f32<-128x512 f32 x1
...
347.58 1.28 ACT L830 ACT_TABLE_LOAD   x1
348.88 0.20 ACT L830 ACTIVATE warm<-zeros 128x1 f32<-128x1 f32 x1
```

The wait at 360.78 went as forecast and the one at 368.37 grew only to 0.97. The two added switches are covered. On their price the Trainium skill (ScalarE: Activation LUTs, What ACT_TABLE_LOAD costs) has about 2.66 us a switch, 1.38 of it drain; here the load starts 0.02 us behind the operation before it, and the next operation 1.3 us after the load's start, in all three switches (347.58, 350.85, 360.08). The measurement decides against the rule. The mis-sized step is the next wait: I had it take back 0.4 of what goes at 360.78, and it took 0.15. And without this edit the new half unit costs 0.6 there (i4), which my sum did not have.

**End, predicted 1.05; measured 1.1 on PE, and 1.5 slower in the span.** Timeline of the changed kernel (compare [rows 9]):

```profile
524.76 0.75 DVE L1411 CUSTOM_DVE_ANT_0 theta<-theta,relu_s,neg_max 128x512 f32<-128x512 f32 x1
...
526.27 0.36 PE L884 MATMUL ps<-v_hi,pT_hi 128*128 128x258 f32 x1 [0.27 <-DVE pT_lo L1425]
...
527.77 1.04 PE L997 MATMUL ps<-ident,theta 128*128 128x128 f32 x8
```

Maximum, transpositions and the new wait are as reckoned, to 0.5 us. The failed step is the sentence "GpSimd then does tile 28, the last gather and tile 29": I asked whether the last gather lands in time and not when GpSimd ends. Tile 30 follows at 531.07 to 532.79, and behind it stands a close of 6.9 us that was in the trace of before, level with the last output there.

**The sum.** 1.2 (front) + 0.3 (the gather at 133) - 1.2 (half units to the third one's first products) + 2.9 (from there through the last expert's first unit) - 0.9 (passage) - 1.1 (PE's end) + 2.6 (close) = 3.8, against the 3.7 in the spans. By this sum the changed kernel without the two events outside my list (2.9 and 2.6) would take 535.3 us, my estimate: faster by 0.3%, with the front as the one term of wrong sign. The loss is shown for the close (e1, g4), for the jump (f1, g1, i4) and for Wq's place in the queue (f2). Only argued is how much of f2's and f4's rest belongs to the bias rows and how much to the six statistics; h1 gives the statistics no more than 0.4.

## What to carry to other kernels

Before an engine's last work is moved later, look at the close of each engine in the last rows of the sequencers, not only at the outputs: here the span ended with the slowest close. Where PE jumps into a loop, read the branch's own duration and the times of the instruction transfers; if a branch is long, move the loop's head into the block where the code ahead of it ends before changing anything else. And a small transfer put ahead of a large one on a queue must be priced by what lands later behind it, not by its own bytes.

## What the runs showed that I had not expected

GpSimd's close takes 6.82 to 6.90 us from its last operation in all the traces read here, whatever that operation is; ScalarE's took 0.6 to 0.7, VectorE's 0.46.

The jump of PE into this loop takes 0.2 to 0.4 us where its block has been there for a while and 3.3 to 4.0 where the block is only asked for at the jump (seven kernels), and with the idle time TensorE may be granted 1.2 GHz: for 3.4 us beside 2.98 idle in the changed kernel, for 6.8 us beside 4.9 idle in g1. The idle time alone does not decide it. e1 fell to 1.2 GHz with 2.42 idle; in e4 the profiled run kept 2.4 GHz behind a wait of 2.67, and by their mean clocks two more of ten did, while the other seven did not. Most kernels without a long jump spread by 0.6 to 1.5 us, but f1 by 2.9, which stays open.

Three transfers of 1 KB land as late as the large ones beside them: they can be used 5.3 to 5.7 us after the start when they are first on their queue, 7.4 to 8.3 when 256 KB stand ahead.
